# Moving three of q's twelve stacking transfers from the SP queue to the ACT queue

## The reference

```python
q = w8a8_linear(layernorm(x), wq, bq)          # 8-bit rows of x and wq, rescaled
k = cond @ wk.T + bk                           # (B, 375, 512)
v = cond @ wv.T + bv
scores = einsum('bhnd,bhld->bhnl', q, k) * inv_sqrt_d + mask   # 16 heads of 32 channels
o = einsum('bhnl,bhld->bhnd', softmax(scores), v)
x = x + w8a8_linear(o, wo, bo)
x = x + experts(layernorm(x))                  # top 2 of 8
```

## Time and profile before

| | |
|---|---|
| median of 3 runs | 1579.15 us (1578.87 to 1583.02) |
| profiled execution | 1580.35 us, its span 1578.6 us |
| PE busy | 1486.5 us, 94% of the span |
| DVE / ACT / POOL busy | 893.2 / 882.1 / 651.3 us |
| granted TensorE clock, mean | 0.973 |
| DMA, mean | 178 GB/s |

### The profile page before, as it was taken

How to read it: one execution, slowest core, us unless ns; L and a number is a source line. 1 busy time by engine, 2 the same in 40 slices (tenths; PEclk the granted TensorE clock), 3 DMA queues, 4 the chain that set the end, 5 groups by cost and what they waited for, 6 DMA issues and landing times. The chain is left out here.

```text
span 1578.6 us, 40115 instructions
## 1 busy us (share of the span) xinstructions
PE 1486.5 (94%) x11594; PEld 1311.1 (83%) x11595; DVE 893.2 (57%) x2366; ACT 882.1 (56%) x2097; POOL 651.3 (41%) x666
## 2 busy tenths in 40 slices
PE   6999999999999999999999999982599999999896
PEld 5888888888888888888888888861599999999895
DVE  7666766667666776667666776656522222222221
ACT  3776667777777677777777677760133333333232
POOL 3233333343323333343333433325355555565453
PEclk9999999999999999999999999995699999999998
DMA  8676677776777677776777677746247776675643
GB/s 259 170 199 185 181 198 214 212 189 183 226 201 202 180 205 207 213 189 183 223 206 197 183 218 192 191 136 228 73 79 186 189 190 129 135 176 115 150 79 48
DMA packets 220123, 281.08 MB, mean 178 GB/s; under 512 B 83568, under 2 KB 164976, under 8 KB 220080
## 3 DMA queue, kind: packets, MB, share of 16 engines
q1 hardware_dynamic: 203088, 246.90, 55.7%
q0 software_dynamic: 16128, 33.30, 12.1%
q10 hardware_dynamic: 864, 0.34, 0.1%
HBM read 118.31 MB, written 66.17 MB: 117 GB/s over the span
## 5 line engine op out<-in xcount | busy, mean ns | idle before, releaser
L331 ACT ACTIVATE probs<-probs,neg_max 112x375 f32<-112x375 f32 x512 | 312.2, 610 | 195.8 <-DVE neg_max L462 190.8
L462 DVE CUSTOM_DVE_ANT_0 probs<-score,neg_mask 112x375 f32<-112x375 f32 x504 | 275.4, 547 | 236.0 <-PE score L611 230.5
L619 PE MATMUL turn<-ident,probs 112*125 112x112 f32 x1536 | 262.9, 280 | 2.7 <-ACT probs_t L318 1.3
L318 ACT ACTIVATE probs_t<-turn 125x336 f32<-125x336 f32 x512 | 225.9, 441 | 69.4 <-PE turn L619 69.0
L619 PEld LDWEIGHTS turn<-ident,probs 112*125 112x125 f32 x1536 | 225.9, 189 | 35.0 <-issue 15.6
L611 PE MATMUL score<-k_stack,q_stack 96*112 96x376 f32 x496 | 200.6, 404 | 3.6 <-DMA q_stack<-q_lo 3.1
L651 PE MATMUL proj<-ctx_hi,wk_hi 128*128 128x376 f32 x512 | 176.0, 344 | 12.5 <-DVE ctx_lo L577 12.5
L1139 DVE TENSOR_TENSOR a_lo<-a_ps,a_hi 128x384 fp32r<-128x384 f32 x63 | 35.2, 558 | 244.3 <-ACT a_hi L1114 232.8
L651 PE MATMUL proj<-ctx_lo,wk_hi 128*128 128x376 f32 x512 | 171.9, 336 | 0.0
L651 PE MATMUL proj<-ctx_hi,wk_lo 128*128 128x376 f32 x512 | 171.7, 335 | 0.0
L656 PE MATMUL proj<-wv_hi,ctx_hi 128*125 128x512 f32 x384 | 151.7, 395 | 1.0 <-DVE v L536 1.0
(11 more groups left out here) (215 smaller groups left out, 3381.6 us busy)
## 6 DMA issues: line engine op xcount, KB each, us to landing
k_stack<-k_hi SPq DMA_DIRECT2D x512, 94.0 KB, 2.4
k_stack<-k_lo SPq DMA_DIRECT2D x256, 94.0 KB, 2.6
ctx_stage<-ctx_t SPq DMA_DIRECT2D x32, 750.0 KB, 5.2
q_stack<-q_hi SPq DMA_DIRECT2D x250, 56.0 KB, 2.0
w_raw_hi<-gate_up_t SPq DMA_DIRECT2D x32, 352.0 KB, 3.1
gate_up_dram_hi<-w_raw_hi SPq DMA_DIRECT2D x32, 352.0 KB, 5.4
gate_up_dram_lo<-w_raw_hi SPq DMA_DIRECT2D x32, 352.0 KB, 5.8
gate_up_hi<-gate_up_dram_hi SPq DMA_DIRECT2D x16, 704.0 KB, 9.4
```

The costliest lines, as they stand in the source:

```text
L318: act.activation(probs_t[:, h % RING_T, :, :], turn[h % 2][0:LC, 0:LT * N].rearrange("p (l n) -> p l n", l=LT), ACT.Copy).then_inc(turned_ ...
L331: act.activation(probs[:, h % DS, :], probs[:, h % DS, :], ACT.Exp, bias=neg_max[:, par % 2, h:h + 1], scale=-1.0, accum_out=total[:, par ...
L462: dve.tensor_tensor_reduce(probs[:, h % DS, :], (last_score[h % 4] if last else score[h % 2])[0:N, 0:L], neg_mask[:, p, :], 1.0, BIG, ALU. ...
L619: mm = pe.transpose(turn[h % 2][0:LC, l * N:(l + 1) * N], probs[:, h % DS, l * LC:(l + 1) * LC], W["ident"][0:N, 0:N])
```

## The change

In slots 11, 13 and 14, behind that slot's softmax, ACT issues one q transfer: (quarter 2, block 0), (3, 0) and (3, 1), all three from `q_hi`. SP leaves these three out of its loop and issues the other nine. Number, size and semaphore of the transfers are as before, in all 31 iterations that have both `has_a` and `has_n`.

```diff
+    ACT_STACKS = {11: (2, 0), 13: (3, 0), 14: (3, 1)}
...
                             for r, src in ((0, q_hi), (1, q_hi), (2, q_lo)):
+                                if (i, r) in ACT_STACKS.values():
+                                    continue
                                 sp.dma_start(q_st[QUARTER * r:QUARTER * r + QUARTER, q, i:H:4, :].bitcast(F32),
                                              src[rows, :, :].bitcast(F32)).then_inc(q_stacked, 16)
...
+                    if h in ACT_STACKS and has_a and has_n:
+                        i, r = ACT_STACKS[h]
+                        need(act, q_hi_made, n + 1)
+                        need(act, scored, H * it)
+                        waited(act)
+                        act.dma_start(q_st[QUARTER * r:QUARTER * r + QUARTER, (par + 1) % 2, i:H:4, :].bitcast(F32),
+                                      q_hi[QUARTER * i:QUARTER * i + QUARTER, :, :].bitcast(F32)).then_inc(q_stacked, 16)
                     if h == 12 and has_a:
```

## The result

The changed kernel takes 1638.37 us (median of 4 runs, 1633.28 to 1646.26) against 1579.01 before (4 runs): the ratio is 1.0379, 95% interval 1.0355 to 1.0404. The forecast was slower, 1623 us with a range of 1596 to 1657. The profiled execution took 1635.17 us, with a span of 1633.3 against 1578.6, 54.7 us more.

What follows compares the result with a forecast made beforehand. PE was taken to bound attention. A 3.3 us chain from exp 14 to the first score, against 1.74, at 31 boundaries adds 48.4 us; less 4.25 us gained, +44 us gives 1623 us, range 1596 to 1657.

Steps and rivals of the forecast that it cites:

- The bound and the period: PE bounds attention; it would wait at each batch's first score, and the period grow from 32.28 to about 33.8 us.
- What is removed: Late q transfers on SP's queue in five periods: its nine issues end 1.95 us earlier, which saves 4.25 us.
- Step 1: On ACT, the transfer issue of slot 13 delays exp 14 by 0.1 us, bounds 0 and 0.2.
- Step 2: From exp 14's start to ACT's slot 14 issue: 0.3 us for two waits and a small instruction.
- Step 3: Slot 14's transfer, issue to landing: 2.0 us plus 0.7 for packets taking turns with SP's, 2.7 us in all.
- Step 4: From the landing of slot 14's transfer to PE's first score: 0.2 us.
- The sum: Exp 14 to first score 3.3 us, 1.56 more than 1.74, at 31 boundaries: 48.4 added, 4.25 removed, net +44 us.
- undisturbed landing: Rival: ACT's transfer lands almost undisturbed by SP's loads, chain 2.4 to 2.85 us, 1595 to 1609 us; chance 0.22.
- Contention: Rival: context, x_in and weight stores hold the engines, landing 3.3 to 4.0 us, time 1641 to 1666; chance 0.15.
- The sequencer did not pass a waiting exp: Rival: ACT's sequencer passes the waiting exp 14, slot 14's issue comes early, only the 4.25 us gain stays, 1575; chance 0.09.

Runs made afterwards that it cites:

- Run 9: Changed kernel with ACT issuing (2,0) in slot 10, (3,0) and (3,1) both in slot 11; 1575.01 us, 0.9978 of the kernel before.
- run 1: Changed kernel without slot 14's issue: ACT issues only in slots 11 and 13, SP the other ten; 1639.71 us, 1.0376 of the kernel before.
- run 2: Changed kernel with SP's loads of the context and x_in put behind the four weight stores; 1593.67 us, 1.0090 of the kernel before.
- run 4: Changed kernel with slot 14's transfer issued ahead of that slot's softmax; 1633.65 us, 1.0340 of the kernel before.
- run 5: Kernel before, no transfer on ACT, SP issuing the context and x_in ahead of the last three q transfers; 1646.66 us, 1.0430.
- run 6: Changed kernel with only x_in put behind the weight stores, the context staying ahead; 1607.21 us, 1.0166 of the kernel before.
- run 7: Changed kernel with ACT's three transfers in slots 10, 11 and 12 instead of 11, 13 and 14; 1583.32 us, 1.0021 of the kernel before.

## Why the prediction was right or wrong

**The bound and the period**: right. PE stalled at the first score of every batch, and by nothing else new of size.

**What is removed**: right. No wait for q_lo is left. Run 9 shows the gain by itself: its first score of the last batch is at 1036.27 us against 1039.93, 3.7 us less, and its median is 3.4 us less, where 4.25 were reckoned.

**Step 1, exp 14's delay of 0.1 us**: it was 0. From slot 14's score to exp 14 it took 1.43 us before and 1.44 after; the issue of slot 13 was over in time.

**Step 2, 0.3 us from exp 14 to the issue**: 0.10 [ACT's rows above]. The sequencer did stand until the exp had started and did not wait for its end; the two new waits and the small instruction are within the 0.10 us.

**Step 3, landing after 2.7 us**: the step that was mis-sized, and its mechanism was wrong. On the mean it was 3.50 - 0.10 - 0.23 = 3.17 us, and 4.3 to 4.9 us for three batches early on, where SP was late and the context was issued only 0.8 to 2.2 us before exp 14. I had the packets take turns at 77 ns; that this gave nearly the right number for the steady part was luck. Runs 1, 2, 4 and 5 show that they stand behind what SP queued earlier. With it fell the sentence that the transfers of slots 11 and 13 land well before the last: that of slot 13 landed 0.5 us before it.

What "earlier" means, the last boundary but one shows. No context is loaded there, ACT's issue of slot 14 comes late (0.43 us behind exp 14), and SP issues a weight store of 352 KB 0.17 us after its start:

```profile
1057.64 0.61 ACTq L405 DMA_DIRECT2D q_stack<-q_hi  x1
...
1057.81 0.37 SPq L233 DMA_DIRECT2D gate_up_dram_hi<-w_raw_hi  x1
```

The store's issue ends first, at 1058.18 against 1058.25. Its packets moved from 1058.6 on and ACT's from 1059.6 on, and the landing took 3.0 us with nothing large issued before it. In run 1's early case it is the other way about: ACT's issue ends at 129.78 and the context's at 129.89, and ACT's packets went first. So it is the end of the issue that fits both, but no run was made to separate it.

The Trainium skill ("DMA: Bandwidth & Descriptors", section "Queues, rings and completion order") has an engine go round its queues and take one packet from each, some 9 to 17 descriptors and 64 at most. The trace does not agree with such turns here, if a packet of the profile is one descriptor, as the prediction took it: 23 of SP's went by for each engine without one of ACT's, which 64 would allow for one transfer, but it was two transfers of SP's that ACT's stood behind, the context and x_in (run 6). The same page's section "Issuing engines are not separate DMA queues" says that issuing from several engines saves only the sequencer's time; runs 5 and 9 agree, with 4.3% lost on one queue alone and 0.2% won from SP's time.

**Step 4, 0.2 us to the score**: right, 0.23 to 0.24 at 26 of the boundaries and 0.09 at five.

**The sum**: 31 x (3.50 - 1.90) = 49.6 us where the steps gave 31 x 3.3 - 59.0 = 43.3. The rest, up to 54.7, is mostly the low clock: the prediction reckoned with no cost of that kind, since the 1 us waits of before had left the clock at 1.00. So two terms were too small, the landing by 0.47 us at each boundary and the clock, put at nothing. The median over four runs is 3.2 us above the profiled one.

**The rivals**: undisturbed landing was not the case, but it is what run 2 made of it. Contention had the size of the early batches (4.3 to 4.9 us to landing), but not their mechanism. The sequencer did not pass a waiting exp: the issues of slot 14 came 0.08 to 0.10 us behind exp 14's start in 30 of the 31 iterations and 0.43 us in one.

## What to carry to other kernels

A transfer that is moved to another engine's queue is bound by two things in this kernel: the instruction before it, for whose start the sequencer stands, and the large transfers that the other queue issued in the microseconds before. So read, before a move, what the donor queue will issue earlier once it is relieved; here SP's relief moved 974 KB right ahead of the transfers that had been taken from it. And look for the slots in which the new engine waits for another one anyway and has no long work behind, for a copy that starts 0.3 us late can reach PE by way of two other engines (run 7). The same three issues cost 3.8% in slots 11, 13 and 14 and gained 0.2% in 10, 11 and 11.

## What the runs showed of the hardware that was not expected

- A 56 KB transfer on ACT's queue moved nothing for 1.4 us and more while SP's queue worked off 974 KB queued earlier; landing 2.0 us with the load behind it, 2.8 to 4.9 with it ahead, and 4.0 to 4.5 from SP's own queue.
- An issue on ACT starts 0.10 us after the start of the activation ahead of it and runs beside it; what it holds back is the next activation, from 0.61 to 0.89 us after the exp in slot 12, and nothing where that one has to wait longer anyway.
- DVE's scaling of x_in (line 420 or 429, 112 x 512) took 0.49 us with nothing on POOL beside it, and beside POOL's subtraction (line 298 or 301) it ended 0.28 us after POOL did: 0.65 us in the kernel before, 0.95 in run 7.
- PE stalls of 1.1 to 3.2 us in nearly every period came with single stretches of 3.4 us at 1.2 GHz: four in the changed kernel's attention, about 1.5 us each, and eleven in run 1. Run 2, with stalls of mostly 0.4 to 0.6 us, had none. What decides when one comes was not tried.
